# Dropping one of two waits before the first gather of each pair of edge groups

## The reference

```python
q = (x @ Wq + bq).reshape(N, H, D)            # H = 8 heads, D = 16
k = (x @ Wk + bk).reshape(N, H, D)
v = (x @ Wv + bv).reshape(N, H, D)
e = (edge_attr @ We).reshape(-1, H, D)
k_e = k[src] + e                              # per edge
v_e = v[src] + e
alpha = einsum('ehd,ehd->eh', q[dst], k_e) / sqrt(D)
a = exp(alpha - segment_max(alpha, dst)[dst])
attn = a / segment_sum(a, dst)[dst]
out = segment_sum(attn[:, :, None] * v_e, dst).reshape(N, 128)
# then a gate with x @ Wskip, a layer norm, relu, x added, and a second layer norm
```

## Time and profile before

| what | value |
|---|---|
| time before, median of 3 runs | 2459.15 us (2456.94 to 2463.15) |
| the profiled execution's own time | 2454.78 us |
| its span | 2453.0 us |
| mean granted TensorE clock | 0.824 of full speed |
| busy: PE, PEld, DVE, ACT, POOL | 1762.1, 1597.7, 1720.9, 805.9, 1492.3 us |
| gathers of the main loop | 1563, of 949 ns on POOL each |
| first and last gather start | 80.4 and 2375.5 us |

### The profile page before, as it was taken

How to read it: one execution, slowest core, us unless ns; L and a number is a source line. 1 busy time by engine, 2 the same in 40 slices (tenths; PEclk the granted TensorE clock), 3 DMA queues, 4 the chain that set the end, 5 groups by cost and what they waited for, 6 DMA issues and landing times. The chain is left out here.

```text
span 2453.0 us, 35080 instructions
## 1 busy us (share of the span) xinstructions
PE 1762.1 (72%) x10434; PEld 1597.7 (65%) x10434; DVE 1720.9 (70%) x2897; ACT 805.9 (33%) x1889; POOL 1492.3 (61%) x1580
## 2 busy tenths in 40 slices
PE   7667777777777777777777776777767776767773
PEld 5566766766666666666667665676667666667662
DVE  6566665666666666677677777777777777777886
ACT  0122222222322332333333333333343334334446
POOL 0466666666666666666666666666666666666650
PEclk9788888888887888888887889879887888887885
DMA  8755656656555555555655555555566566656641
GB/s 302 243 186 185 198 179 201 193 181 199 184 166 171 167 185 169 171 182 163 186 176 167 188 173 178 179 174 186 171 198 191 183 196 191 194 178 200 198 144 48
DMA packets 231807, 449.01 MB, mean 183 GB/s; under 512 B 42082, under 2 KB 151752, under 8 KB 218974
## 3 DMA queue, kind: packets, MB, share of 16 engines
q1 hardware_dynamic: 156304, 241.36, 30.1%
q0 software_dynamic: 75312, 205.36, 27.9%
HBM read 404.57 MB, written 41.99 MB: 182 GB/s over the span
## 5 line engine op out<-in xcount | busy, mean ns | idle before, releaser
L784 POOL DMA_INDIRECT kv<-kv_tab,src_all x1498 | 1421.8, 949 | 706.7 <-issue 409.7
L1020 PE MATMUL sum_ps<-wv,hot_en 128*128 128x136 f32 x3136 | 563.7, 309 | 367.5 <-issue 345.7
L1020 PEld LDWEIGHTS sum_ps<-wv,hot_en 128*128 128x128 f32 x3136 | 464.7, 209 | 420.2 <-issue 413.3
L908 PE MATMUL q_all<-q_win,hot_ne 128*128 128x128 f32 x3136 | 452.5, 306 | 3.2 <-DVE prod L1505 1.9
L908 PEld LDWEIGHTS q_all<-q_win,hot_ne 128*128 128x128 f32 x3136 | 443.6, 225 | 7.0 <-issue 6.2
L1505 DVE TENSOR_TENSOR prod<-q_all,kve 128x1024 f32<-128x1024 f32 x196 | 240.0, 1225 | 288.4 <-remote 273.6
L1494 DVE TENSOR_TENSOR kve<-kv,e_ps 128x768 f32<-128x768 f32 (+1 forms) x392 | 407.4, 1080 | 7.1 <-issue 5.3
L1168 ACT ACTIVATE wt_ps<-logit,used_b 128x64 f32<-128x64 f32 x196 | 62.2, 318 | 1061.1 <-issue 862.5
L893 PE MATMUL e_ps<-we,tab_buf 128*128 128x128 f32 x1568 | 307.2, 361 | 112.2 <-issue 88.1
L893 PEld LDWEIGHTS e_ps<-we,tab_buf 128*128 128x128 f32 x1568 | 282.7, 268 | 141.4 <-issue 134.0
L893 PE MATMUL e_ps<-we,ea 128*128 128x128 f32 x1568 | 318.6, 377 | 72.9 <-issue 51.8
(11 more groups left out here) (151 smaller groups left out, 1096.1 us busy)
## 6 DMA issues: line engine op xcount, KB each, us to landing
ea<-eaT SPq DMA_DIRECT2D x49, 1024.0 KB
row_b<-rel_row SPq DMA_DIRECT2D x98, 512.0 KB
tab_buf<-eaT SPq DMA_DIRECT2D x49, 1024.0 KB
kv<-kv_tab,src_all POOLq DMA_INDIRECT x1498
q_win<-q_tab SPq DMA_DIRECT2D x252, 64.0 KB
sum_tab<-sums SPq DMA_DIRECT2D x251, 59.5 KB
kv_tab<-tab_buf SPq DMA_DIRECT2D x33, 384.0 KB, 3.9
logit<-sum_tab SPq DMA_DIRECT2D x49, 136.0 KB
```

The source lines that it names most:

```text
L784: pool.indirect_dma_start(out=head_rows(q) if u == t == 0 else kv[:, s, t, :], out_offset=None, in_=kv_tab[:, :], in_offset=bass.IndirectO ...
L908: mm = pe.matmul(q_ps[u][:, t * P:(t + 1) * P], hot_ne[:, 2 * par + u, t * P:(t + 1) * P], q_win[:, 2 * par + min(u, parts(q) - 1), :], st ...
L1020: mm = pe.matmul(sum_ps[1 if wide else u][:, 0:AC], hot_en[:, 2 * par + u, t, :], wv[:, 2 * par + u, t, :], start=(t == 0 and not (wide an ...
```

## The change

The first gather of a pair no longer waits for `q_ok` of two pairs back. Its other wait, for the key sum that read the head's place three pairs ago, stays. No instruction is added, removed or put in another order, on any engine; on POOL one awaited semaphore per pair is gone for pairs 2 to 195.

```diff
                 for u in range(2):
                     s = 2 * par + u
                     for t in range(TILES_G):
-                        if q >= 2 and u == 0 and t == 0:
-                            pool.wait_ge(q_ok, 2 * (q - 2) + 2)
-                            if q >= 3:
-                                pool.wait_ge(kve_ok, kve_head(q - 3))
+                        if q >= 3 and u == 0 and t == 0:
+                            pool.wait_ge(kve_ok, kve_head(q - 3))
                         elif q >= 2 and t == 1 - u:
                             pool.wait_ge(kve_ok, kve_count(2 * q + u - 4))
```

## The result

The changed kernel takes 2824.53 us (median of 4 runs, 2808.43 to 2838.97), the kernel before 2458.34 us (4 runs) beside it: a ratio of 1.1485, 95% interval 1.1445 to 1.1525. It is 366 us slower. The profiled execution has a span of 2837.2 us against 2453.0.

The account below looks back on a forecast made before the run. The loop was taken as bound by a ring of POOL, PE's completions and DVE: 0.8 x 13.08 + 0.2 x 15.7 = 13.6 us per pair, +1.85 x 189 = +350 us, 2809 us; whole range 2440 to 3210.

Parts of the forecast that it names:

- The ring, and what ends a wait: Main loop: POOL, PE's completions, DVE, POOL set the period; completions surely come only when back-to-back gathers end.
- The single train: Eight gathers, then POOL held 3.36 us at the second gather for a key sum: 13.08 us per pair, +1.33.
- The price of a double train: Two pairs' 16 gathers back to back plus delays on DVE: 31.3 us, or 15.7 per pair, +3.9.
- never to be seen: Sign in the loop: the product starts 1.8 us or more after a train's end, never inside one.
- The rival of leaking results: PE's completions get out inside long trains: 12.3 us per pair, +108 us, 2567 us; chance 0.18.
- How many doubles: Share of the loop's pairs in trains of 16: one in five, giving 13.6 us per pair.
- The delay from a train's end: From the last of 16 gathers to the product: 2.9 us, the middle of 1.77 and 4.04.
- More and longer waits of the head's key sum: Sign on DVE: the head's key sum (L1489 before) waits more often and longer; no size given.
- The tail: After the last gather, products follow by 9.73 us with DVE alone the bound; expected unchanged.
- The pause is pure loss: Rival: POOL's 2.04 us wait at the head goes, completions come as now: 2134 us at best; chance 0.18.
- PE is really busy until then: Rival: PE works until 1217.4, recorded ends are too early; the wait only moves, 2459 us; chance 0.08.

Follow-up runs that it names:

- experiments 2 and 3: Changed kernel plus POOL memsets before each head, no `q_ok` wait: pause 2.20 us, ratio 1.0036; pauses 0.91, 1.27, 1.63 us, ratios 1.1184, 1.1017, 1.0406.
- 4 and 5: First: changed kernel, gathers replaced by ordinary DMAs of the same bytes, ratio 0.7642; second: kernel before, gathers of 512 B rows, half the bytes, ratio 1.0012.
- plain: Changed kernel, each indirect gather replaced by an ordinary DMA of 128 consecutive 1 KB rows: 1899.39 us against 2483.77, ratio 0.7642.

## Why the prediction was right, and where only its sum was

The measured 2824.5 us lies 16 us from the predicted 2809, and the mechanism is the one forecast: the pause at the head goes, and a longer one before the second gather takes its place. That the number is so close is luck, since two errors in the sum cancel.

- **The ring, and what ends a wait.** Right. No "remote" wait stands before the heads, POOL stops before second gathers, for key sums. That PE's completions are held by the train of gathers was read from the trace; experiments 2 and 3 show that a long enough stretch without gathers gives the time back without a wait for `q_ok`, and 4 and 5 that the bytes don't matter.
- **The single train.** Right in size: 3.27 us of hold where 3.36 was forecast, 13.0 us per pair where 13.08.
- **The price of a double train.** Too high: 27.7 us for two pairs (19.75 + 8.00) against 31.3. The step that failed is "the key sum after that stands behind a product on DVE, whose `q_ok` waits for a train's end". In 55 of the 80 such trains the second product started inside the train, 13 us after its start on average, as at 924.11, which the prediction had named as never to be seen; the pause behind them was 7.0 us. In the other 25 it came 2.1 us after the train's end, where 2.9 was forecast, and the pause was 10.1 us against the forecast's 2.9 + 8.7 = 11.6. The rival of leaking results was thus half right: they leak, but mostly at steps of 1.42 us and not for all of PE's work. In the stretch shown, POOL was in the end let go by L1550, which waited for PE's sums until the hold ended. That wait, 304.7 us over the run, stands in no part of the prediction.
- **How many doubles.** Far too few: one pair in five was chosen, 160 of 191 were measured. With the measured prices the forecast's share would have given 0.8 x 13.0 + 0.2 x 13.9 = 13.2 us per pair, 2730 us; with its own price the measured share would have given 15.3, some 3120. The choice rested on "the loop's own trains are all of eight", but those were cut at eight by the very wait that the change removes, so they were no evidence. The row that bore on it was half of the key sums not waiting for `e_ok`.
- **The whole.** 80 x 27.7 + 31 x 13.0 = 2619 us for 191 pairs, where before 191 x 11.75 = 2244 us: +375 of the 384 us between the two spans. The unpredicted start, where 33 gathers ran on end, is in the rest.
- **The delay from a train's end.** For the whole hold the middle taken for 16 gathers, 2.9 us, was close: 16 x 1.42 - 19.75 = 3.0, and PE's sums came out 22.5 to 23.0 us after the train's start. But the product, for which it was used, seldom waited that long (the bullet on the double train).
- **More and longer waits of the head's key sum.** Wrong: L1487 waited 79.0 + 17.7 us, where L1489 had waited 229.7 + 62.3. The time moved to the product and to L1550.
- **The tail.** Unchanged, as said. These two products stand at the end of the gathers, where those of the earlier trace rows stood:

```profile
2760.38 1.23 DVE L1503 TENSOR_TENSOR prod<-q_all,kve 128x1024 f32<-128x1024 f32 x1 [0.20 <-DVE kve L1492]
...
2770.11 1.22 DVE L1503 TENSOR_TENSOR prod<-q_all,kve 128x1024 f32<-128x1024 f32 x1 [0.20 <-DVE kve L1492]
```

They are 9.73 us apart, as in the earlier trace rows. One more follows 11.55 us later in both kernels.

- **"The pause is pure loss"** and the rule of the Trainium skill's "Trainium Kernel Development and Optimization" behind it (Best Practices, overlap DMA with compute) fail where the hold exists: issuing the gathers earlier cost 15%. **"PE is really busy until then"** is refuted too. The Trainium skill's "Perfetto Trace Analysis" (Tensor Engine Instruction) says that a matmul's reported end is an estimate, but plain, with every matmul in place and the same bytes moved, has no such wait, though at a higher granted clock (0.964).

What is open: what the 1.42 us of a gather are spent on, and why PE has to wait for them; what in an indirect gather makes the hold and whether its price goes by rows; why the hold was absent in one of five comparisons; and whether a pause of 1.76 us, which by 9.72 + 1.76 = 11.48 against 11.75 would beat the kernel before where the hold exists, does so. No version that computes the layer's own result beat it there.

## What to carry to other kernels

A wait that isn't needed for the data can still be needed for the time. Before you drop one, ask what happens during the pause that it makes, and look on every engine for work that starts only when the pause comes. A long "remote" wait whose supposed source is recorded as finished microseconds before is the sign: line the release times up with what another queue was doing. And a pattern that the trace shows throughout (trains of eight) is no evidence of what follows when the thing that makes the pattern is taken away.

## What the runs showed of the hardware

- Gathers issued back to back held PE's completions until about 1.42 us per gather from the first: 11.4 us for 8, 22.7 for 16, 34.2 for 24, 46.7 for 33. Halving the bytes of a row didn't change it (ratio 1.0012); ordinary DMAs of rows of the same size didn't show it.
- In a long train PE itself nearly stops: from 917 to 931 us it ran one to four matmuls at a time, these groups starting 0.7 to 3.5 us apart. With the hold, stretches of 0.71 us between the starts of two matmuls are common (259 and 237 times in the two kernels); without it they are rare (4 to 10 times).
- The kernel before took 2458, 2484, 2458 and 2484 us in the four comparisons with the hold and 2113 us in one without. Ratios taken with the hold don't carry over to a run without it: a pause that brought the changed kernel to 1.00 with the hold (2.20 us) costs time without it (1.91 us: 1.14), where the kernel before needs no pause.
